# A graph network on one core: 21 dense tiles instead of 16, one stream of gathered chunk groups, neighbour weights in the table rows

## The reference, cut to what matters

```
deg = segment_sum(1, dst);  dinv = deg ** -0.5;  norm = dinv[src] * dinv[dst]
h = layernorm(x)
for l in range(5):
    edge_fea = concat([attr[:, 3:] @ ew1[l], attr[:, 0:3] @ ew2[l]])      # 128 + 128 columns
    agg = segment_sum(norm[:, None] * (h[src] + edge_fea), dst)
    h = relu(concat([h, agg]) @ mlp_w[l] + mlp_b[l])                      # mlp_w is 512 x 256
    h = batchnorm(h) * bn_g[l] + bn_b[l];  if l != 4: h = relu(h)
x = x + h
x = x + shared_ffn(layernorm(x)) + top2_of_8_experts(layernorm(x))
```

## Time and profile before

| | us |
|---|---|
| median of 3 executions (lowest, highest) | 7248.25 (7244.58, 7257.27) |
| the profiled execution | 7252.64 |
| its span, from the first to the last instruction | 7250.9 |
| before layer 0 | 0 to 733 |
| layer 0 up to the first transpose back | 733 to 1773 |
| the five stages of sums | 1040, 978, 985, 984, 981 |
| experts and the rest | 5906 to 7251 |

### The profile page before, as it was taken

How to read it: one execution, slowest core, us unless ns; L and a number is a source line. 1 busy time by engine, 2 the same in 40 slices (tenths; PEclk the granted TensorE clock), 3 DMA queues, 4 the chain that set the end, 5 groups by cost and what they waited for, 6 DMA issues and landing times. The chain is left out here.

```text
span 7250.9 us, 110910 instructions
## 1 busy us (share of the span) xinstructions
PE 5200.5 (72%) x26233; PEld 3225.8 (44%) x26234; DVE 2062.7 (28%) x4788; ACT 976.8 (13%) x2579; POOL 3458.6 (48%) x3614
## 2 busy tenths in 40 slices
PE   1304677777677776777775777776777778999997
PEld 1203344444334443344443444443444447888876
DVE  7806333334122223222223222222222243100012
ACT  2505000002000002000002000011000022222221
POOL 3771555554555554555554555545555524100013
PEclk9956788887788887888887889887888889999998
DMA  5443555554545555455554555545555541111112
GB/s 199 52 85 101 141 144 141 143 143 133 147 142 149 148 148 149 143 147 147 149 150 147 150 147 150 149 124 167 148 149 147 148 136 59 53 58 46 58 47 87
DMA packets 437672, 919.83 MB, mean 127 GB/s; under 512 B 121026, under 2 KB 260063, under 8 KB 425007
## 3 DMA queue, kind: packets, MB, share of 16 engines
q0 software_dynamic: 214352, 627.20, 30.7%
q1 hardware_dynamic: 169342, 159.61, 7.7%
q10 hardware_dynamic: 53856, 131.73, 5.8%
HBM read 779.74 MB, written 138.52 MB: 127 GB/s over the span
## 5 line engine op out<-in xcount | busy, mean ns | idle before, releaser
L1101 POOL DMA_INDIRECT sets<-rows,index x2960 | 2813.9, 951 | 2223.9 <-ACT index L1129 960.5
L1561 PE MATMUL bank<-sets,row_out 128*128 x3280 | 1406.5, 453 | 767.2 <-issue 439.5
L1610 PE MATMUL bank<-resid,arena 128*128 128x512 bf16 x3920 | 1376.9, 394 | 74.8 <-issue 74.8
L1612 PE MATMUL bank<-sets,arena 128*128 128x256 bf16 x3920 | 1100.2, 281 | 82.2 <-issue 81.8
L1562 PE MATMUL bank<-sets,row_out 128*128 x3280 | 1036.7, 316 | 125.1 <-issue 123.2
L1561 PEld LDWEIGHTS bank<-sets,row_out 128*128 x3280 | 365.1, 111 | 1255.9 <-issue 1055.6
L1970 PE MATMUL bank<-sets,arena 128*128 128x256 f32 x2480 | 630.6, 387 | 58.7 <-issue 29.5
L1610 PEld LDWEIGHTS bank<-resid,arena 128*128 128x128 bf16 x3920 | 397.2, 101 | 540.7 <-issue 139.6
L1129 ACT ACTIVATE index<-arena x740 | 152.3, 206 | 3226.7 <-SPq L1040 1594.4
L1296 DVE SCALAR_TENSOR_TENSOR row_out<-bank,neg_base,arena 128x512 f32 x528 | 396.3, 751 | 632.8 <-issue 488.1
L1970 PEld LDWEIGHTS bank<-sets,arena 128*128 128x128 f32 x2480 | 479.2, 194 | 135.4 <-issue 38.8
(11 more groups left out here) (344 smaller groups left out, 4809.3 us busy)
## 6 DMA issues: line engine op xcount, KB each, us to landing
arena<-dense ACTq DMA_DIRECT2D x80, 1184.0 KB
sets<-rows,index POOLq DMA_INDIRECT x2960
arena<-dense ACTq DMA_DIRECT2D x81, 384.0 KB
rows<-resid SPq DMA_DIRECT2D x56, 512.0 KB, 3.0
dense<-feat_t SPq DMA_DIRECT2D x16, 1568.2 KB, 16.2
rows<-sets SPq DMA_DIRECT2D x56, 256.0 KB, 3.4
expert_in<-zero SPq DMA_DIRECT2D x14, 1024.0 KB
expert_out<-zero SPq DMA_DIRECT2D x14, 1024.0 KB
```

Source lines behind the costliest of these rows:

```text
L1101: pool.indirect_dma_start(got0_words[:, j, 0:W0 // 2] if first else got[:, j, :], None, rows0 if first else rows, bass.IndirectOffsetOnAxi ...
L1561: pe.matmul(to, ones, rows_here[:, ds(from_here + j * wide, 2 * D)], start=start, stop=False)
L1610: pe.matmul(bank[:, 5, 0:2 * D], dense_in_sb[:, u * P:(u + 1) * P], high_parts[:, u, :], start=u == 0, stop=False)
L1612: mm = pe.matmul(bank[:, 5, D:2 * D], dense_in_sb[:, u * P:(u + 1) * P], low_parts[:, u, :], start=False, stop=u == NT - 1)
```

## The change

Of the 49 tiles 21 (tiles 1 to 21) are dense and 28 (tile 0 and tiles 22 to 48) are gathered. They are handled in 7 units of 7 slots: gathered tiles in slots 0, 2, 4, 6, dense ones in 1, 3, 5. All data by tile (`resid`, `feat_t`, `dinv`) is kept in slot order. The gathered tiles are one stream of aligned groups of 4 chunks: a group in which one tile ends and the next begins is multiplied twice (`border`), and no column is gathered again for alignment. `mlp_w`'s lower half (the neighbour weights) is applied to each row before it enters the table (L1728's transposes become fp32 matmuls of 256 columns; in block 2 likewise for layer 0), so that the transposed sum is added by DVE to `h @ w1 + b` in `feat_t` (`place`), and `mix` has two blocks left. The edge term is one bf16 matmul of 256 columns a tile (`edges_of`); in layer 0 DVE adds it in `take`. The dense matrix comes in four parts with a load each. The window has 19 edges a partition (19 scatter rounds of 21: 6, 3, 10), the dense cells are zeroed from a 512-wide constant, layer 0's edge windows keep 20. The lower weights are loaded while a layer's sums run (`load_w2`), the upper behind them (`load_w1`), and PE no longer waits for `applied` before a layer. The input rows are loaded by ACT, the final stores by SP tile by tile with constants.

```diff
-WIN = 20
+WIN = 19
+EWIN = 20
...
-    NTR = NT // 3
-    NU = NTR + 1
+    UN = 7
+    US = NT // UN
+    ND = 3 * UN
+    NG = NT - ND
+    FIRST_D = 1
...
-    ROUNDS = (7, 10, WIN)
+    ROUNDS = (6, 9, WIN)
...
+                pe.wait_ge(w2_in, 48)
+                for p in range(NPAIR):
+                    if p >= 4:
+                        pe.wait_ge(row0_rest, p - 3)
+                    for u in range(pair_width(p)):
+                        t = p * 2 + u
+                        for k in range(KD):
+                            mm = pe.matmul(bank[:, ROW0_BANKS[p % 4], u * D:(u + 1) * D], feat_t[:, k, t * P:(t + 1) * P],
+                                           mix_w[:, KD + k, :], start=k == 0, stop=k == KD - 1)
+                    mm.then_inc(row0_made, 1)
...
-        DENSE_PARTS = (0, 12, 24, 34, NT)
+        DENSE_PARTS = (0, 12, 24, 36, NT)
...
+                    def load(u, j, part):
+
+                        i = u * 3 + j
+                        if part < 3:
+                            wait_past(act, dense_used, (l * ND + i) * 3 + (part - 2))
+                        else:
+                            wait_past(act, sum_done, l * NT + u * US + 2 * j - 1 + (j > 0))
+                        gated(act)
+                        a, b = DENSE_PARTS[part:part + 2]
+                        act.dma_start(dense_in_sb[:, a * P:b * P], dense_cells(i, a, b)).then_inc(dense_in[part], 16)
...
+                        here = feat_t[:, :, nodes(u * US + c)]
+                        dve.tensor_tensor(here, bank[:, 2, 0:D].rearrange("p (k n) -> p k n", k=KD), here, ALU.add)\
+                            .then_inc(sum_placed, 1)
...
+                    def chunk(to, ones, rows_here, j, start=False, stop=False):
...
+                        a = j * HW
+                        pe.matmul(to[:, 0:2 * D], ones, rows_here[:, a:a + 2 * D], start=start, stop=False)
+                        return pe.matmul(to[:, D:2 * D], ones, rows_here[:, a + 2 * D:a + HW], start=False, stop=stop)
...
+                    def edges_of(u, c, b):
+
+                        return pe.matmul(bank[:, b, 0:D], edge_t[:, ds((u * 3 + c // 3) * P, P)], edge_v[:, c % 3, :],
+                                         start=False, stop=True)
+
+                    def border(u, c, b, b_2):
+
+                        at, rows_here = group_here()
+                        ones = hot_flat[:, ds(at, K * P)]
+                        ones_2 = hot_2_flat[:, ds(at, K * P)]
+                        for j in range(K):
+                            mm = chunk(bank[:, b, :], ones[:, j * P:(j + 1) * P], rows_here, j, stop=first and j == K - 1)
+                        if not first:
+                            mm = edges_of(u, c, b)
+                        mm.then_inc(sum_done, 1)
...
+                        for j in range(K):
+                            mm = chunk(bank[:, b_2, :], ones_2[:, j * P:(j + 1) * P], rows_here, j,
+                                       start=not first and j == 0)
...
+                    def mix(u, b, f):
+
+                        off, n = BATCHES[b]
...
+                        for k in range(KD):
+                            mm = pe.matmul(bank[:, MIX[f], 0:n * P], mix_w[:, k, f * P:(f + 1) * P],
+                                           feat_t[:, k, nodes(u * US + off, n)], start=k == 0, stop=k == KD - 1)
...
+                    def unit(u, head):
+                        dense_sums(u, 0, 0, () if head else {0: lambda: turn(u - 1, 5)})
+                        inner(u * 4, 0)
+                        dense_sums(u, 0, 1, () if head else {0: lambda: turn(u - 1, 6)})
+                        if head and not first:
+                            pe.wait_ge(edge_v_set, l)
                             gated(pe)
+                        border(u, 0, 0, 1)
+                        dense_sums(u, 0, 2, {1: lambda: mix(u, 0, 0), 5: lambda: mix(u, 0, 1)})
+                        light_or_heavy(u * 3 + NG, 1)
+                        dense_sums(u, 0, 3, {0: lambda: turn(u, 0)})
+                        inner(u * 4 + 1, 1)
+                        dense_sums(u, 1, 0, {0: lambda: turn(u, 1)})
+                        border(u, 2, 1, 0)
+                        dense_sums(u, 1, 1)
+                        light_or_heavy(u * 3 + (NG + 1), 0)
+                        dense_sums(u, 1, 2, {0: lambda: turn(u, 2)})
+                        inner(u * 4 + 2, 0)
+                        dense_sums(u, 1, 3)
+                        border(u, 4, 0, 1)
+                        dense_sums(u, 2, 0, {0: lambda: turn(u, 3), 8: lambda: mix(u, 1, 0), 11: lambda: mix(u, 1, 1)})
+                        light_or_heavy(u * 3 + (NG + 2), 1)
+                        dense_sums(u, 2, 1, {0: lambda: turn(u, 4)})
+                        inner(u * 4 + 3, 1)
+                        dense_sums(u, 2, 2)
+                        dense_sums(u, 2, 3)
+                        border(u, 6, 1, 0)
...
-                                    mm = pe.transpose(bank[:, ROW_BANKS[t // 2 % 4], ds(u * D + k * P, P)],
-                                                      feat_t[:, k, (t + u) * P:(t + u + 1) * P], ident[:])
+                                    at = feat_t[:, k, (t + u) * P:(t + u + 1) * P]
+                                    to = bank[:, ROW_BANKS[t // 2 % 4], u * D:(u + 1) * D]
+                                    if final:
+                                        mm = pe.transpose(to[:, k * P:(k + 1) * P], at, ident[:])
+                                    else:
+                                        mm = pe.matmul(to, at, mix_w[:, KD + k, :], start=k == 0, stop=k == KD - 1)
```

More of the change, by code:

```diff
@@ L200, in build @@
[L200 to L208 removed]
+        deg_now = stage(NT)
@@ L220, in build @@
[L220 to L226, removed]
+        clashes = sb("clashes", [P, ND])
+        clashes_b = sb("clashes_b", [P, ND], BF16)
+        starts = stage(ND)
+        starts_i = sb("starts_i", [P, ND], I32)
+        fits = sb("fits", [P, ND])
@@ L834, in _ @@
+                act.wait_ge(edge_0_made, 1)
+                for h in range(2):
+                    act.activation(edge_0[:, h * 2:h * 2 + 2, :], bank[:, h, :].rearrange("p (a d) -> p a d", d=D), ACT.Copy)
             @block.gpsimd
@@ L995, in in_layers @@
             body(L - 1, False, True)
-        def in_blocks(engine, body):
-            def four(v):
-                for s in range(4):
-                    body(v * 4 + s, s, BT, v)
-            loop(engine, NB // 4, four)
-            body(NB - 1, 0, 1, NB // 4)
         def counter(engine, name):
@@ L1206, in layer @@
+                    with placed(act, mybir.EngineType.Activation, 1, UN, 0) as u:
+                        unit(u, False)
+                    relu(UN - 1, 0)
+                    relu(UN - 1, 1)
+                    if not final:
+                        first_loads(l + 1)
                     act.wait_ge(var_ready, l + 1)
@@ L1715, in layer @@
+                    zeroed(0)
+                    unit(0, True)
+                    with placed(pe, mybir.EngineType.PE, 1, UN, 0) as u:
+                        unit(u, False)
                     if first:
                         pe.reg_add(turns_h, turns_h, R)
-                    turn(NT - 1)
-                    for f in range(KD):
-                        mix_h(NT - 1, 1, f)
+                    turn(UN - 1, 5)
+                    pe.matmul(bank[:, 0, 0:WB], zero[:, 0:P], zero[:, 0:WB], start=False, stop=True)
@@ L2333, in build @@
         added = sem("added")
-        stored = [sem(f"stored{u}") for u in range(4)]
-        def fours(engine, body):
-            def four(i):
-                for u in range(4):
-                    body(i * 4 + u, u, i, P)
-            loop(engine, NT // 4, four)
-            body(NT - 1, 0, NT // 4, LAST)
+        stored = sem("stored")
         with nc.Block() as block:
```

1270 lines of the change are left out of this document (724 added, 546 removed).

## The result

The changed kernel takes **7040.6 us** (median of 4 runs, 7035.0 to 7050.3) against 7251.1 beside it: ratio **0.971**, 95% interval 0.969 to 0.973. 6725 was forecast: the direction came, less than half of the size. The profiled execution has a span of 7037.6 us at a granted TensorE clock of 0.879 (0.853 before).

The account below looks back on a forecast made before the run. PE sets the pace, losing 238 us to standstill and 147 to half clock a stage. 7252.6 - 705 (sums) + 60 (rows) - 32 (layer starts) + 8 (edge rows) + 140 (before layer 0) = 6723.6, said 6725; range 6450 to 7180.

Parts of the forecast that it names:

- The stages' work: PE's work in a stage of sums: 590 us after the change, against 593 before.
- The standstill: PE standing still in a stage of sums: 155 us after, 238 before.
- the half clock: PE time lost to the half clock in a stage of sums: 96 us after, 147 before, following the standstill.
- Layer 0: Layer 0's sums: given the same saving of 141 us as the mean of the other layers' stages.
- Block 1: Before layer 0: more scatters and windows, but no wait for zeroed cells before counting; +15 us (0 to 30).
- Block 2: Before layer 0: 63 scatters instead of 48 and 98 PE matmuls; +15 us (0 to 100).
- rival C: Before layer 0: two waits beside POOL's scatters, in blocks 2 and 3, add 88 us: 6813 us; chance 0.16.
- Block 3: Before layer 0: 210 scatters instead of 160 (+64) and 105 lookup steps behind them (+47), together +111 us.
- Rows between layers: Transposes become fp32 matmuls and PE the bound: 1.71 us a pair at full clock, +15 us four times, +60.
- Rival A: Stages of sums: standstill and half clock stay at 238 and 147, a stage is 975 us: 7394 us; chance 0.12.
- B: Stages of sums: stalls belong to the jump back at the body's end, a stage is 758 us: 6309; chance 0.15.
- D: A dense tile that doesn't fit is gathered: five more groups, 6.5 us for each and layer; chance 0.02.

Follow-up runs that it names:

- e4: The changed kernel with three of the four edge products left out of layer 0's `take`: 7008.6 us, 0.970 of the kernel before.
- h1: The changed kernel with wide zero source, two products a dense pair in layer 0, no gathers in layers 1 to 4: 5968.6 us, 0.821.
- e1: The changed kernel with the dense matrices zeroed from a wide source (6273 bf16 instead of 369 repeated 17 times): 6934.2 us, 0.960 of the kernel before.
- f3: The changed kernel with wide zero source and block 3's lookups and window loads as loops, on a chip with pauses: 7055.3 us, 0.952.
- e3: The changed kernel with wide zero source and scatter rounds 9, 0, 10 instead of 6, 3, 10: 6974.9 us, 0.964 of the kernel before.
- g2: The changed kernel with wide zero source and two products a dense pair in layer 0, on a chip without pauses: 0.958 of the kernel before.
- g5: The changed kernel with wide zero source and two products a dense pair in layer 0, run again on a chip without pauses: 0.956.
- e7: The changed kernel with two products instead of three a dense pair in layer 0, narrow zero source, chip without pauses: 5721.8 us, 0.966.
- f2: The changed kernel, unchanged, run again on a chip with pauses: 7097.1 us, 0.961 of the kernel before.

## Why the prediction was wrong

**The stages' work, 590 us**: right. Without gathers a stage is 609 to 611 us to its last transposed sum, with 12 of standstill.

**The standstill, 155, and the half clock, 96**: right in size for layers 1 to 4 (858 - 669 = 189, at the upper end of the 125 to 190, and 669 - 590 = 79; together 268 for 251, so 858 for 841; with the starts, 58 us of the miss). Its cause was left at "sequencer and fetch", taken as a property of the code's shape. It needs indirect DMAs beside it and a chip of one kind, and it grows with the products streamed: 268 us on 3536 records in layer 1 are 76 ns each, and layer 0's (1008 less some 600 of work) on 5171 are 79 ns. The 59 us of waiting for landings, which I let go, shrank to 20 here; on the chip without pauses they were 39. I counted 0.947 us of POOL for a gather, which holds it for 1.25 with the gap behind it.

**Layer 0, "I give it the same 141"**: the first failing step, 112 us. The number of PE's products stood in the diff: a dense pair of layer 0 went from two products to three, and 784 pairs became 1029. Its products rose from 4108 to 5171, those of the other layers only from 3400 to 3536. I counted columns, which hardly change, and `take`'s steps, which e4 shows to be worth 8 to 16 us. Before, layer 1 lost 399 us on 3400 products (117 ns each) and layer 0 some 440 on 4108 (107). Per product the loss fell by about 30% in both, and layer 0 spent that on 1063 products more. Why it fell no run tells. h1's 937 would have been -103, so that the products account for about two thirds of the 112 and some 40 us stay open.

**Block 1, +15**: the second failing step, +147 measured (285 to 432). I took the zeroing at nothing, since the counting no longer waits for it, and did not price its packets. That wait went to POOL: 21 matrices at 151 GB/s land at 288, and six rounds of scatters stand behind. e1 gives 113 us of it back (block 1 ends at 319); in later executions of the wide source it ended at 378 to 380 where each scatter took longer (last section), and at 372 in f3, whose scatters were fast but whose counting crawled from 230 to 300 us (DVE busy 17 of 70 us, 67 in e1).

**Block 2, +15 (0 to 100)**: +51, in the range, by the starving that rival C named; e3 shows 68 us of it. **Block 3, +111**: +108, right. C was priced at two waits of 44 us on straight code; the first came as 68, the second not, and the 132 us of the zeroing weren't in it.

**Rows between layers**: 44.2 us for the 25 pairs, 1.77 a pair for 1.7, PE solid at 0.96; +53 for +68. PE became the bound of this stretch as forecast.

**Rival A** is refuted (a stage gave back 134), **B** too: a stage took 858 us and not 758, and without gathers the same jumps leave 12 us of standstill in a stage. **D** didn't happen: 2480 gathers, 399 scatters.

## What to carry to other kernels

Beside indirect DMAs count an engine's instructions, not only its columns or bytes: here 1029 products more in a stage, with not a column more, cost 62 us on one kind of chip and 16 on the other. A wait that is taken from one engine is still somewhere; price the transfer behind it by its packet size, and name who waits now. Before a pause is read as a property of the code, run the same kernel on a second chip: the changed kernel's stage took 858 us on one and 659 on another.

The best version measured is the change with the wide zero source and two products a dense pair in layer 0 (g2, g5): 0.958 and 0.956 of the kernel before on chips without pauses, where e7 with the narrow source had 0.966. On a chip with pauses it was run only in h1, which leaves the gathers out; there f3, the wide source with looped lookups, had 0.952 beside f2's 0.961, and e1, the wide source alone, 0.960 at another time. 937 us in layer 0 promise some 80 us more, which is not measured as a whole.

## What the runs showed that I had not expected

- Two kinds of chip: 7234 to 7402 and 5915 to 5933 us for one kernel. One chip had 7234 us at one time and 7402 at another. What differs between the kinds is open; the packets of POOL's indirect DMAs took 0.165 us on the mean in the kernel after and 0.161 in e7 (27.0% and 32.4% of 16 engines' span over 184544 packets), so they are alike.
- The starving builds up: in block 2 PE ran 17 us freely beside the scatters before it fell to 4 products in 21 us, and ACT's loop made three passes before they grew. What fills up in this time, and through what POOL's indirect DMAs reach other engines' instructions, no run tells.
- A scatter is 0.96 us beside idle engines and 2.77 beside block 1's counting. POOL's timeline of g2, as the counting ends:

```profile
230.30 2.77 POOL L439 DMA_INDIRECT dense<-sets  x1 [0.30 <-issue]
```

```profile
291.22 0.96 POOL L439 DMA_INDIRECT dense<-sets  x1 [0.30 <-issue]
```

 In e1 they took 1.2 on the mean (56 us for 47) beside the same counting, and block 1 ended 60 us earlier than in g2. The Trainium skill ("SBUF — State Buffer", section "SBUF: two separate sides") says that POOL can't write descriptors while DVE runs in a two-port mode. No row here names the mode of DVE's steps; the 2.77 would fit, and the 1.2 of e1, with DVE as busy (70 of 70 us from 160 to 230 in both), show that it doesn't come every time.
